# A two-layer graph network: two DRAM tables laid out in four quarters

## The chip, the cores and the metric

The kernel runs on one core of a Trainium2 chip. The metric is the device time of one execution in microseconds. The kernel before takes 4035.39 us, the median of 3 runs (4032.98 to 4035.66).

## The reference

12500 nodes with 256 features, 200000 edges (`src`, `dst`) sorted by `dst`, one weight per edge. Cut to what is computed:

```python
# layer 0: 2 projections, 4 heads of 32, attention-weighted sum over edges, norm per head
feat = relu(einsum('nd,ohdk->ohnk', x, W) + b)
att_s, att_n = leaky(feat[0] . a_self), leaky(feat[1] . a_neigh)
msgs = (att_s[:, row] + att_n[:, col]) * adj_vals * feat[1][:, col, :]
agg = segment_sum(msgs, row)
h0 = concat(norm32([feat[0], agg]) * scale + offset)
x = layernorm(x + h0)
# layer 1: one message per edge, sum over edges, update
messages = relu(concat([x[row], x[col]]) @ W_msg + b_msg)
aggregated = segment_sum(messages, col)
h = relu(concat([x, aggregated]) @ W_upd + b_upd)
x = layernorm(x + layernorm(h) * gamma + beta)
```

In the call `row` is `src` and `col` is `dst` for the first layer's arguments, as `edge_index = stack([src, dst])` is for the second.

## The kernel before

Rows are worked on in 98 tiles of 128 nodes, taken as 49 pairs of 256 rows (`NP` = 49). `x1` below is the x after layer 0. The kernel has three stages; each engine runs its own program, and they meet through semaphores.

The first stage projects the rows and sorts the edges' messages into a DRAM table `d_m`.

The second stage is a loop over `E_END` groups. A group gathers five message rows per partition from `d_m` (L781, by GpSimd's indirect DMA, four buffers `GB`), weighs them (ScalarE L996, VectorE L1753 and L1756) and adds them up by matmul (L1305). Eight groups make a pair. Beside the groups two row pipelines run. `own` makes the first half of the new rows and stores them in `d_xp` (L670). `node`, steps 0 to 21 of a pair after its sums are there, loads them again (step 0, L675, into one of two buffers `X1`; first used at L1849), adds the second half, normalises, and then stores three things. Step 14 (L678) stores the normalised rows plus `bet`, for use as residual, in `d_x1`. Step 15 (L684) stores the transposed rows `XT1` (made at L1042) in `d_y`. Step 17 (L681) stores the product with the first half of `W_msg` in `d_p`. All these DMAs are issued by the SP queue in the order of its program, each after its wait: a late wait holds back all that stand behind it. The step's group is given by the table `AT_B`: one step a group, and for the last pairs two or three steps a group.

At the turn every engine waits in `stored_b` until all stores of `d_xp`, `d_x1`, `d_p` and `d_y` have landed. Only then may the gathers from `d_p` begin.

The third stage is a loop over 403 groups of four gathers (L795, from `d_p`, eight buffers `G1`, so that gathers may run seven groups ahead). VectorE adds the looked-up part of the other end (L1913; the lookup is the matmul L1339), ScalarE applies relu (L1111), the matmul L1327 sums by one-hot, and VectorE adds the sums to `big` (L1903). Beside it runs `node1`, 18 steps for each pair, placed by `AT_F`: step 0 loads the pair's transposed rows (L707, into one of two buffers `XTL`; used by the matmul L1360 in step 2) and, for a pair four ahead, again into `XTQ` (L710, used at L1370 in steps 5 and 6). Step 7 loads the residual rows (L713, buffer `XR`, used by VectorE at L1944 in step 11), and step 17 stores the output (L717). The SP queue also loads the tables of the one-hots, 384 KB every three groups (L698, `spread`).

Both tables are written once and read once or twice. The two shapes on the DRAM side now are

```python
def pair(t, j):
    return t[bass.ds(j * 256, 256), :].rearrange("(b p) c -> p b c", p=128)   # d_x1: 128 x 2 x 1 KB
d_y[p * 128:(p + 1) * 128, :]                                                 # d_y: 128 x 2 KB
```

The SBUF side has 128 partitions in both. If a check of the edges fails, a slow path computes everything in another way; it uses `d_x1` too and does not run here.

Of the kernel before, what the change touches and what calls it, by code (L numbers as in the profile page):

```python
# [15 lines left out]
NP = 49  # L16
# [119 lines left out]
def owned(g):  # L136

    for j in (g // 8 - 1, g // 8):
        if 0 <= j < NP and g - 8 * j < 12:
            yield j, g - 8 * j  # L140
# [24 lines left out]
QL = 4  # L165
# [4 lines left out]
def pq(p, n):  # L170

    return p + min(p, QL) + n
# [7 lines left out]
def dense(g, at):  # L180

    return at.get(g, ())
# [30 lines left out]
def gnn(nc, x, xT, src, dst, ew, srcB, dstB, ewB, dst0, W0, b0, att, scale, offset, Wm, bm, Wu, bu, gam, bet, cst, out):  # L213
    ctx = ExitStack()
    with ctx:
# [5 lines left out]
        def S(name):  # L221
            name = SHARED[name][0] if name in SHARED else name
            if name not in sems:
                sems[name] = ctx.enter_context(nc.semaphore("q_" + name))
            return sems[name]

        def base(name):

            return SHARED[name][1] if name in SHARED else 0

        def waitn(e, name, v):

            if not isinstance(v, int) or v > 0:
                e.wait_ge(S(name), v + base(name))

        def dram(name, shape, dt=f32):
            return nc.dram_tensor(name, shape, dt).ap()
# [12 lines left out]
        d_b = dram("d_b", (3, 768), bf16)  # L250
        d_xp = dram("d_xp", (NROW, 256))
        d_x1 = dram("d_x1", (NROW, 256))
        d_p = dram("d_p", (NROW, 256))
        d_q = dram("d_q", (NROW, 256))
        d_y = dram("d_y", (NP * 128, 512))
        d_loc = dram("d_loc", (NS, 128), bf16)
        srcF, dstF = (t.rearrange("a b -> (a b)").rearrange("(a b c) -> a b c", b=128, c=1) for t in (srcT, dstT))

# [53 lines left out]
        def q4(ap):  # L312
            return ap.rearrange("p (a b) -> p a b", a=4)
# [117 lines left out]
        X1 = [take(2, 256) for _ in range(2)]  # L431
        XN = take(2, 256)
        XT1 = take(4, 128)
# [23 lines left out]
        XTL = [take(4, 128) for _ in range(2)]  # L457
# [5 lines left out]
        XR = scr[:, 4096:4608].rearrange("p (a b) -> p a b", a=2)  # L463
        XTQ = q4(w0[:, :, :].rearrange("p a b -> p (a b)"))
# [25 lines left out]
        def pair(t, j):  # L490

            return t[bass.ds(j * 256, 256), :].rearrange("(b p) c -> p b c", p=128)

        def sm(g, a, n):
            return small[:, g % 4, a:a + n]

# [41 lines left out]
        def stored_b(e):  # L538
            stored_own(e)
            stored_p(e)  # L540
            e.wait_ge(S("b_s1"), 16 * NP)
            e.wait_ge(S("b_s4"), 16 * NP)
# [14 lines left out]
        def _(e):  # L557
# [91 lines left out]
            def columns(j):  # L649

                waitn(e, "d_mm", j - 2)
                n = 256 if j < NP - 1 else 128 + LASTR
                e.dma_start(XT0B[j % 3][:, :, 0:n], xT.rearrange("(k p) n -> p k n", p=128)[:, :, j * 256:j * 256 + n])\
                 .then_inc(S(f"d_xt{j % 3}"), 16)
            columns(0)
            columns(1)
            for g in range(E_END):
                for j, o in owned(g):
                    if o == 0 and j + 2 < NP:
                        columns(j + 2)  # L660
                    if o == 5:
                        waitn(e, f"d_st{j % 2}", 16 * (j // 2))
                        if j < NP - 1:
                            e.dma_start(X0[j % 2], pair(x, j)).then_inc(S(f"d_in{j % 2}"), 16)
                        else:
                            e.dma_start(X0[j % 2][:, 0, :], x[j * 256:j * 256 + 128, :]).then_inc(S(f"d_in{j % 2}"), 16)
                            e.dma_start(X0[j % 2][0:LASTR, 1, :], x[j * 256 + 128:N, :]).then_inc(S(f"d_in{j % 2}"), 16)
                    if o == 11:
                        waitn(e, "d_x", j + 1)
                        e.dma_start(pair(d_xp, j), X0[j % 2]).then_inc(S(f"d_st{j % 2}"), 16)  # L670
                for p, o in dense(g, AT_B):
                    if o == 0:
                        waitn(e, f"d_st{p % 2}", 16 * (p // 2 + 1))
                        waitn(e, "b_s1", 16 * (p - 1))
                        e.dma_start(X1[p % 2], pair(d_xp, p)).then_inc(S(f"b_in{p % 2}"), 16)  # L675
                    if o == 14:
                        waitn(e, "b_xb", p + 1)
                        e.dma_start(pair(d_x1, p), X1[p % 2]).then_inc(S("b_s1"), 16)  # L678
                    if o == 17:
                        waitn(e, "b_pq", pq(p, 0) + 1)  # L680
                        e.dma_start(pair(d_p, p), PB).then_inc(S("b_s3"), 16)  # L681
                    if o == 15:
                        waitn(e, "b_xt", p + 1)
                        e.dma_start(d_y[p * 128:(p + 1) * 128, :], XT1.rearrange("p a b -> p (a b)")).then_inc(S("b_s4"), 16)  # L684
            stored_b(e)
            waitn(e, "b_x", NP)
            waitn(e, "b_mm", pq(NP, 0))
# [7 lines left out]
            def spread(n):  # L695

                waitn(e, "f_ot", BL * (n - 1))
                e.dma_start(LBC[n % 2], d_loc[4 * BL * n:4 * BL * (n + 1), :].rearrange("(o a) b -> o (a b)", o=1).to_broadcast([128, BL * 512]))\  # L698
                 .then_inc(S(f"f_l{n % 2}"), 16)
            spread(0)  # L700
            for g in range(F_END):
                if g % BL == 0 and BL * (g // BL + 1) < NG:
                    spread(g // BL + 1)
                for p, o in dense(g, AT_F):
                    if o == 0:
                        waitn(e, "g_mm", p - 1)
                        e.dma_start(XTL[p % 2].rearrange("p a b -> p (a b)"), d_y[p * 128:(p + 1) * 128, :]).then_inc(S(f"g_in{p % 2}"), 16)  # L707
                        if p + QL < NP:
                            waitn(e, "g_qm", p)
                            e.dma_start(XTQ.rearrange("p a b -> p (a b)"), d_y[(p + QL) * 128:(p + QL + 1) * 128, :]).then_inc(S("g_xq"), 16)  # L710
                    if o == 7:
                        waitn(e, "g_add", p)
                        e.dma_start(XR, pair(d_x1, p)).then_inc(S("g_x"), 16)  # L713
                    if o == 17:
                        waitn(e, "g_n2", 2 * (p + 1))
                        if p < NP - 1:
                            e.dma_start(pair(out, p), UH[p % 3]).then_inc(S(f"g_st{p % 3}"), 16)  # L717
                        else:
                            e.dma_start(out[p * 256:p * 256 + 128, :], UH[p % 3][:, 0, :]).then_inc(S(f"g_st{p % 3}"), 16)
                            e.dma_start(out[p * 256 + 128:N, :], UH[p % 3][0:LASTR, 1, :]).then_inc(S(f"g_st{p % 3}"), 16)  # L720
# [144 lines left out]
        def _(e):  # L865
# [142 lines left out]
            def own(j, o):  # L1008
                if o == 1:
                    waitn(e, "d_mm", j + 1)  # L1010
                    e.activation(FS(j), FS(j), ACT.Relu).then_inc(S("d_re"), 1)
                if o == 5:
                    waitn(e, "d_rv", j)
                    waitn(e, "d_xc", j + 1)
                    e.activation(SQ0, FS(j), ACT.Square).then_inc(S("d_s2"), 1)
                if o == 7:
                    waitn(e, "d_var", j + 1)
                    e.activation(SD(j), sm(j % 2, 56, 8), ACT.Sqrt).then_inc(S("d_sq"), 1)
# [51 lines left out]
            def node1(p, o):  # L1070
# [12 lines left out]
                if o == 7:  # L1083
                    waitn(e, "g_v1", p + 1)
                    e.activation(sm(p, 100, 2), sm(p, 98, 2), ACT.Sqrt).then_inc(S("g_sq"), 1)
                    q = p + QL
                    if q < NP:
                        waitn(e, "g_qm", p + 1)
                        e.activation(big[:, 2 * q + 1:2 * q + 3, :], q2(PG[:, :]), ACT.Copy).then_inc(S("g_qc"), 1)
                if o == 9:  # L1090
                    waitn(e, "g_a1", 2 * (p + 1))
                    waitn(e, "g_rn", p + 1)
                    for b in range(2):
                        e.activation(u[:, b, :], u[:, b, :], ACT.Identity,
                                     bias=sm(p, 104 + b, 1), scale=sm(p, 102 + b, 1)).then_inc(S("g_n1"), 1)
# [1045 lines left out]
```

## Time and profile before

| | us |
|---|---|
| median of 3 timed runs | 4035.39 |
| lowest, highest | 4032.98, 4035.66 |
| span of the profiled execution | 4403.8 |

The profiled execution has no other time than its span, from its first to its last instruction; it is 368.4 us longer than the median of the timed runs. Busy in the span: TensorE 87%, VectorE 77%, ScalarE 63%, GpSimd 56%. A matmul's end is modelled, so TensorE's share is rough. Gathers run on the DMA queue q0 and move 359.18 MB, the SP queue's transfers on q1 and move 343.13 MB. "Share of 16 engines" is the time that the queue's packets took, against 16 DMA engines (here called rings) working all the time; it can pass 100% in a short stretch, since packets overlap. A DMA issue on SP (SPq) is a short instruction; its transfer runs afterwards. Tile names leave out numbers: `d_x` in a row is `d_x1`.

### The profile page before, as it was taken

The page shows a single profiled execution, that of the slowest core. Times are in us where ns is not written, and L with a number is a line of the kernel's source. Part 1 is how long each engine was busy: PE and PEld are TensorE (multiplying, and loading weights), DVE is VectorE, ACT ScalarE, POOL GpSimd, SP SyncE. Part 2 cuts the span into 40 slices and gives each one's busy share as a digit, 9 for nine tenths or more (in the row PEclk, how much of TensorE's full clock was granted, in tenths as well). Part 3 has the DMA queues.
Part 4 walks back from the last instruction along what each step waited for, and adds up shares of the span by engine and source line. Part 5 has one row for each costly group of instructions (what it writes and reads, how often), then busy time and mean ns, then how long its engine had stood idle before and what let it go on. Part 6 is the DMA issues. An engine that isn't in the chain of part 4 may idle for free.

```text
span 4403.8 us, 85804 instructions
## 1 busy us (share of the span) xinstructions
PE 3810.6 (87%) x26341; PEld 3176.6 (72%) x26341; DVE 3380.9 (77%) x7638; ACT 2779.1 (63%) x7247; POOL 2477.9 (56%) x2585
## 2 busy tenths in 40 slices
PE   4999999899999999956888888878888888888886
PEld 4999999788888888845666666666666666666665
DVE  7999999799999999955666666666666666666666
ACT  4888888777777777744555555555555555555554
POOL 2653655344455555536666666666666666666662
PEclk8999999999999999988899999999999989999998
DMA  5776544567777777743444444444444444444442
GB/s 133 243 231 226 190 189 188 197 191 206 209 209 209 209 209 208 206 141 110 127 142 129 136 127 140 132 130 136 131 132 136 135 131 131 128 129 139 131 131 72
DMA packets 344434, 707.82 MB, mean 161 GB/s; under 512 B 58153, under 2 KB 201334, under 8 KB 343954
## 3 DMA queue, kind: packets, MB, share of 16 engines
q0 software_dynamic: 114912, 359.18, 29.2%
q1 hardware_dynamic: 229074, 343.13, 23.1%
q8 instruction: 225, 3.69, 0.4%
q14 instruction: 223, 1.83, 0.1%
HBM read 507.96 MB, written 195.74 MB: 160 GB/s over the span
## 4 chain that ended last, share of the span: by engine, by line
PE 44%; DVE 29%; issue 11%; another core or an unknown queue 9%; ACT 2%; DVEq 2%; DMA 2%; SPq 1%; POOL 0%; ACTq 0%; POOLq 0%
PE ps L1327 11%; PE ps L1339 10%; DVE big L1903 7%; PE ps L1157 6%; DVE scr L1753 4%; PE ps L1305 4%; DVE arena L1913 3%; DVE arena L1756 3%; PE ps L1219 2%; PE ps L1164 2%; PE ps L1230 2%; PE ps L1188 2%; DVE scr L1756 1%; PE ps L1147 1%
## 5 line engine op out<-in xcount | busy, mean ns | idle before, releaser
L795 POOL DMA_INDIRECT arena<-d_p,tabs x1612 | 1543.0, 957 | 890.8 <-issue 457.3
L1913 DVE TENSOR_TENSOR arena<-arena,ps 128x512 f32<-128x512 f32 x806 | 527.0, 683 | 760.9 <-remote 503.8
L1327 PE MATMUL ps<-arena 128*128 128x256 f32 x3224 | 897.3, 419 | 240.1 <-DVE big L1903 174.2
L1111 ACT ACTIVATE arena<-arena 128x1024 f32<-128x1024 f32 x403 | 425.7, 1056 | 1004.8 <-DVE arena L1913 956.3
L1339 PE MATMUL ps<-big,scr 128*128 x3224 | 840.3, 401 | 219.6 <-DVE arena L1913 134.4
L1327 PEld LDWEIGHTS ps<-arena 128*128 128x128 f32 x3224 | 627.7, 205 | 424.2 <-ACT arena L1111 192.3
L1339 PEld LDWEIGHTS ps<-big,scr 128*128 128x128 f32 x3224 | 641.9, 202 | 356.9 <-issue 261.1
L1903 DVE SCALAR_TENSOR_TENSOR big<-big,tabs,ps 128x256 f32 x1612 | 767.8, 476 | 105.7 <-DVE big L1903 47.7
L781 POOL DMA_INDIRECT arena<-d_m,scr x392 | 531.2, 1355 | 564.0 <-DVE arena L1756 220.8
L1305 PE MATMUL ps<-arena,scr 128*128 128x256 f32 x2620 | 614.9, 384 | 10.5 <-DVE arena L1756 10.3
L1305 PEld LDWEIGHTS ps<-arena,scr 128*128 128x128 f32 x2620 | 483.7, 190 | 93.2 <-issue 32.9
L996 ACT ACTIVATE arena<-arena 128x128 f32<-128x128 f32 x1310 | 410.7, 389 | 206.2 <-PE ps L1305 132.7
L1064 ACT ACTIVATE arena<-cstb,tabs 128x128 f32<-128x128 f32 x1612 | 508.8, 386 | 2.3 <-DMA d_p<-arena 2.3
L1157 PE MATMUL ps<-arena,scr 128*128 128x132 bf16 x4860 | 377.0, 221 | 6.5 <-ACT arena L910 4.2
L1753 DVE TENSOR_TENSOR scr<-scr,arena 128x640 f32<-128x640 f32 x392 | 320.7, 818 | 3.2 <-issue 3.1
L1157 PEld LDWEIGHTS ps<-arena,scr 128*128 128x128 bf16 x4860 | 305.1, 97 | 10.5 <-ACT arena L910 6.7
L1305 PE MATMUL ps<-scr 128*128 128x256 f32 x1300 | 307.3, 383 | 3.8 <-DVE scr L1756 3.7
L747 POOL DMA_INDIRECT arena<-d_ts,arena x108 | 135.3, 1253 | 296.0 <-PE ps L1157 274.5
L910 ACT ACTIVATE arena<-ps 128x396 f32<-128x396 f32 x540 | 277.9, 515 | 19.4 <-issue 10.3
L916 ACT ACTIVATE scr<-ps 128x512 bf16<-128x512 f32 (+1 forms) x432 | 251.1, 581 | 52.2 <-PE ps L1164 48.9
L1305 PEld LDWEIGHTS ps<-scr 128*128 128x128 f32 x1300 | 239.6, 190 | 44.3 <-issue 15.2
L1067 ACT ACTIVATE arena<-arena 128x512 f32<-128x512 f32 x403 | 253.8, 630 | 12.7
(285 smaller groups left out, 5753.3 us busy)
## 6 DMA issues: line engine op xcount, KB each, us to landing
d_m<-arena SPq DMA_DIRECT2D x108, 603.0 KB
arena<-d_loc SPq DMA_DIRECT2D x135, 384.0 KB
d_m<-arena SPq DMA_DIRECT2D x108, 402.0 KB
arena<-d_p,tabs POOLq DMA_INDIRECT x1612
arena<-in_xT_dram SPq DMA_DIRECT2D x96, 256.0 KB
d_xp<-arena SPq DMA_DIRECT2D x49, 256.0 KB, 3.3
arena<-d_xp SPq DMA_DIRECT2D x49, 256.0 KB
d_x<-arena SPq DMA_DIRECT2D x49, 256.0 KB
```

The lines of the kernel that those rows point to most:

```text
L781: e.indirect_dma_start(out=GB[g % 4].rearrange("p a b -> p (a b)"), out_offset=None, in_=runs_m, in_offset=bass.IndirectOffsetOnAxis(ap=TI ...
L795: e.indirect_dma_start(out=G1[j % 8][:, k, :], out_offset=None, in_=d_p, in_offset=bass.IndirectOffsetOnAxis(ap=tabS[:, j, k:k + 1], axis= ...
L996: a = e.activation(SW[g % 3][:, s, 0:128], v[:, 0:128], ACT.Copy, scale=v[:, FW + 1:FW + 2])
L1064: s = e.activation(OH1[j % 4][:, k, :], iota, ACT.Square, bias=tabN[:, j, k:k + 1])
L1111: e.activation(G1[g % 8], G1[g % 8], ACT.Relu).then_inc(S("f_re"), 1)
L1157: m = e.matmul(PS[6 + (NE * q + k) % 2][:, (cc - c0) * FW:(cc - c0 + 1) * FW], SELT[q % 2][:, cc, :], FWN[q % 2][:, i * FW:(i + 1) * FW], ...
L1305: m = e.matmul(AC(p)[:, h, :], OHW[g % 3][:, s, :], SW[g % 3][:, s, :], start=first, stop=end)
L1327: m = e.matmul(turn(H, AB)[:, k * 256:k * 256 + 256], OH1[(j - 2) % 4][:, 2 * h + k, :], G1[(j - 2) % 8][:, 2 * h + k, :], start=True, sto ...
L1339: m = e.matmul(turn(H, QB)[:, k * 256:k * 256 + 256], OT1[j % 2][:, 2 * h + k, :], big[:, ts[2 * h + k] + 1, :], start=True, stop=True)
L1753: e.tensor_tensor(OHW[g % 3], IT[t % 3].unsqueeze(1).to_broadcast(b5), v[:, :, FW].unsqueeze(2).to_broadcast(b5), ALU.is_equal).then_inc(S ...
L1903: e.scalar_tensor_tensor(big[:, ts[k], :], big[:, ts[k], :], tabK[:, j - 3, k:k + 1], turn(H, AB)[:, (k % 2) * 256:(k % 2) * 256 + 256], A ...
L1913: e.tensor_tensor(v, v, q2(turn(2 * j + h, QB)[:, :]), ALU.add).then_inc(S("f_m"), 1)
```

## The change

A new DRAM table `d_xr` takes the residual rows in the fast path, `d_x1` stays for the slow path. `d_y` and `d_xr` have the shape [4, 49 * 32, 512]: partitions 0 to 31 of each pair lie in the first quarter, 32 to 63 in the second, and so on. `quarters(t, p)` is the DRAM side of pair p's copy, [4, 32, 512]. The SBUF side is the buffer as [128, 512]; for the residual the two rows of a partition now lie side by side, 2 KB in one piece. The number of stores issued so far is counted in `kept` while the program is written out, and L675 waits for all of them.

```diff
+        d_xr = dram("d_xr", (4, NP * 32, 512))
...
-        d_y = dram("d_y", (NP * 128, 512))
+        d_y = dram("d_y", (4, NP * 32, 512))
...
+        def quarters(t, p):
+
+            return t[:, p * 32:(p + 1) * 32, :]
...
+            kept = 0
...
                     if o == 0:
                         waitn(e, f"d_st{p % 2}", 16 * (p // 2 + 1))
-                        waitn(e, "b_s1", 16 * (p - 1))
+                        waitn(e, "b_s1", 16 * kept)
                         e.dma_start(X1[p % 2], pair(d_xp, p)).then_inc(S(f"b_in{p % 2}"), 16)
                     if o == 14:
                         waitn(e, "b_xb", p + 1)
-                        e.dma_start(pair(d_x1, p), X1[p % 2]).then_inc(S("b_s1"), 16)
+                        kept += 1
+                        e.dma_start(quarters(d_xr, p), X1[p % 2].rearrange("p a b -> p (a b)")).then_inc(S("b_s1"), 16)
...
-                        e.dma_start(d_y[p * 128:(p + 1) * 128, :], XT1.rearrange("p a b -> p (a b)")).then_inc(S("b_s4"), 16)
+                        e.dma_start(quarters(d_y, p), XT1.rearrange("p a b -> p (a b)")).then_inc(S("b_s4"), 16)
...
-                        e.dma_start(XTL[p % 2].rearrange("p a b -> p (a b)"), d_y[p * 128:(p + 1) * 128, :]).then_inc(S(f"g_in{p % 2}"), 16)
+                        e.dma_start(XTL[p % 2].rearrange("p a b -> p (a b)"), quarters(d_y, p)).then_inc(S(f"g_in{p % 2}"), 16)
                         if p + QL < NP:
                             waitn(e, "g_qm", p)
-                            e.dma_start(XTQ.rearrange("p a b -> p (a b)"), d_y[(p + QL) * 128:(p + QL + 1) * 128, :]).then_inc(S("g_xq"), 16)
+                            e.dma_start(XTQ.rearrange("p a b -> p (a b)"), quarters(d_y, p + QL)).then_inc(S("g_xq"), 16)
                     if o == 7:
                         waitn(e, "g_add", p)
-                        e.dma_start(XR, pair(d_x1, p)).then_inc(S("g_x"), 16)
+                        e.dma_start(XR.rearrange("p a b -> p (a b)"), quarters(d_xr, p)).then_inc(S("g_x"), 16)
```

## Rows read from the trace of the kernel before

**Rows 1.** Busy time by stretch: us, then each engine's, clock, DMA share, GB/s.
```profile
821.00:1946.00 1125.00, 1083.98 (x5800) 908.33 (x5800) 1065.71 (x2604) 803.05 (x2566) 531.18 (x393) 0.99 0.69 201
1946.00:4404.00 2458.00, 1975.39 (x7976) 1540.69 (x7976) 1554.18 (x3605) 1336.95 (x2902) 1542.96 (x1612) 0.91 0.43 129
...
1380.00:1822.00 442.00, 436.21 (x2343) 364.76 (x2341) 431.55 (x1063) 324.13 (x1041) 222.96 (x160) 1.00 0.71 209
```

**Rows 2.** Waits: of ScalarE's L996 in 821 to 1946 us, and before L1756.
```profile
ACT arena L996 <- DMA arena<-d_m,scr: 69.1, 60, 8.0
ACT scr L996 <- DMA arena<-d_m,scr: 22.5, 29, 2.2
...
  ACT arena L996: 4.5, 8
  ACT scr L996: 1.5, 4
```

**Rows 3.** SP's DMA issues of one pair: start us, us; then the next pair's first.
```profile
1501.72 0.38 SPq L678 DMA_DIRECT2D d_x<-arena  x1
1503.59 0.38 SPq L670 DMA_DIRECT2D d_xp<-arena  x1
1504.91 0.34 SPq L684 DMA_DIRECT2D d_y<-arena  x1
1506.82 0.38 SPq L675 DMA_DIRECT2D arena<-d_xp  x1
...
1523.80 0.38 SPq L678 DMA_DIRECT2D d_x<-arena  x1
```

**Rows 4.** DMA queue from 32 to 34 us: packets, MB, share of 16 engines.
```profile
q1 hardware_dynamic: 88, 0.04, 7.3%
```

**Rows 5.** The same from 1527 to 1528.5 us.
```profile
q1 hardware_dynamic: 497, 0.58, 107.5%
q0 software_dynamic: 1, 0.00, 0.0%
```

**Rows 6.** Lines L795 and L1913: ns min/median/max, first and last start; L1913's waits.
```profile
L795 POOL DMA_INDIRECT arena<-d_p,tabs x1612: 940/946/1394, 1946.0 to 4339.0; - x180
...
L1913 DVE TENSOR_TENSOR arena<-arena,ps x806: 678/681/690, 1954.6 to 4369.9; 128x512 f32<-128x512 f32 x162
...
  remote: 503.8, 136
  PE ps L1339: 199.1, 106
```

**Rows 7.** Timeline around the last pairs of the second stage; idle time in brackets.
```profile
1923.85 0.40 SPq L678 DMA_DIRECT2D d_x<-arena  x1
1924.62 0.34 SPq L684 DMA_DIRECT2D d_y<-arena  x1
...
1927.79 0.47 SPq L670 DMA_DIRECT2D d_xp<-arena  x1
1930.29 0.38 SPq L675 DMA_DIRECT2D arena<-d_xp  x1
...
1932.95 0.43 DVE L1849 TENSOR_TENSOR arena<-arena 128x256 f32<-128x256 f32 x1 [2.96 <-DMA arena<-d_xp]
...
1937.23 0.37 SPq L678 DMA_DIRECT2D d_x<-arena  x1
1938.46 0.34 SPq L684 DMA_DIRECT2D d_y<-arena  x1
...
1942.98 0.37 SPq L681 DMA_DIRECT2D d_p<-arena  x1
```

**Rows 8.** Timeline of the last two pairs' loads of d_y and their use.
```profile
4358.74 0.47 SPq L707 DMA_DIRECT2D scr<-d_y  x1
...
4361.85 1.13 PE L1360 MATMUL ps<-wut,scr 128*128 128x256 f32 x4 [1.55 <-ACT scr L1076]
...
4383.83 0.47 SPq L707 DMA_DIRECT2D scr<-d_y  x1
...
4386.74 2.05 PE L1360 MATMUL ps<-wut,scr 128*128 128x256 f32 x4 [3.52 <-DMA scr<-d_y]
```

## The prediction

> **What bounds the kernel now.** I read the busy time by stage first [rows 1]. The span has three stages. Sorting lasts to 821 us. The second stage (first layer's edges, and pair by pair the rows of the new x) lasts to 1946 us, and the third (second layer's edges, and pair by pair the output) fills the rest. The change touches only the SP queue's stores in the second stage and its loads in the third. In the steady part of the second stage VectorE works 431.55 of 442 us [rows 1], so it sets the pace. The DMA rings are 71% busy there, the highest of any stage, so this is the place where a slower transfer can hurt. In the third stage the rings are 43% busy and no engine is full; the loop between TensorE, VectorE and ScalarE is the limit.
>
> Then I read who waits for gathers in the second stage. ScalarE's weighing (L996) waits for a landing gather 89 times, 91.6 us in all, and VectorE's product (L1756), which takes ScalarE's result, waits for ScalarE only 12 times, 6.0 us [rows 2]. So lateness of a gather is nearly all absorbed on ScalarE; 6.0 / 91.6 = 6.5% reaches the engine that sets the pace.
>
> Then the SP queue of one pair [rows 3]. The store of the residual rows (L678) is followed 1.87 us later by a store of d_xp (L670), 1.32 us later by the store of transposed rows (L684), and 1.91 us later by a load (L675) that waits for both the d_xp store and the residual stores. A pair takes 1523.80 - 1501.72 = 22.08 us (L678 to L678).
>
> **What the layout does to one transfer.** Both sides of these copies have 128 rows now: 128 partitions and 128 rows of 2 KB in d_y; 128 partitions with two 1 KB pieces each for the residual. Afterwards the DRAM side is [4, 32, 512]. The trace has transfers whose outermost size does not divide into 16: the stores of 101 rows of 512 B in the start-up. In the stretch where one of them runs alone, 0.04 MB move in 2 us at a ring share of 7.3%, about 22 GB/s: one ring of 16 works [rows 4]. Where nothing but transfers of the normal form run, 0.58 MB move in 1.5 us, 387 GB/s on all rings [rows 5]. Nothing shows an outermost size of 4 at this size; the bounds are 16 rings, as now (256 KB / 387 GB/s = 0.68 us), and one ring (256 KB / 22 GB/s = 11.9 us). I take four rings, 88 GB/s: 2.98 us, because the 101-row transfer shows that the shape decides how many rings work. That is 2.3 us longer per transfer, and four rings hold four times the work while twelve hold none.
>
> The Trainium skill (DMA: Bandwidth & Descriptors, section "Why a DMA increments its semaphore by 16 and not by 1") says the same of shapes: the ring count is the largest number up to 16 that divides the slowest dimension of both sides, and on this queue the lowest-numbered rings are used. By that all five changed transfers sit on the same four rings. One ring for 101, a prime, agrees with it; which rings they are no row shows. Its table "Rules for kernel authors" warns against an outermost size below 16, and thus speaks against this change.
>
> The number of transfers is 49 stores of d_xr, 49 stores of d_y, 49 + 45 loads of d_y and 49 loads of d_xr. The residual rows go from 256 pieces of 1 KB to 128 of 2 KB. That saves at best a few tenths of a microsecond of ring time against the 2.3 us added, and I cost it at zero. SP's issue time (0.38 us for L678, 0.34 us for L684 [rows 3]) can move either way by its own size; SP waits for other engines most of the time, so it counts nothing. The new wait of L675 (for all residual stores issued) is the same number as before for all pairs but the last two (after the steps of the last pairs are spread differently, `kept` is p instead of p - 1); queued behind it are the loads of x and x^T and the store of d_p.
>
> **Sum, the ends.** Here a transfer stands on the path.
> - End of the second stage. For the last pair the load L675 (1930.29) follows the d_xp store (1927.79), and VectorE waits 2.96 us for it at 1932.95 [rows 7]. The two long stores before (1923.85 and 1924.62) hold their rings for 2 x 2.98 = 5.96 us after the first begins. The d_xp store comes 3.94 us after the first, so its share on these rings is 2.0 us late. Bounds 0 and 4.6 (both excesses in full). I take 2.0.
> - Turn of the stages. The last two long stores are issued at 1937.23 and 1938.46, and the d_p store for which all gathers wait at 1942.98 [rows 7], 5.75 us after the first: 0.2 us late.
> - End of the kernel. The last load of d_y is issued at 4383.83; TensorE waits 3.52 us and starts at 4386.74 [rows 8], so +2.3. For the pair before, the load is issued at 4358.74 and used at 4361.85, 3.11 us later, after a wait for ScalarE [rows 8]. A load that took 2.91 us takes 5.2: +2.1. Together 4.4, bounds 0 and 4.6.
>
> Ends: 2.0 + 0.2 + 4.4 = 6.6 us.
>
> **Sum, middle of the second stage.** Per pair the SP queue moves seven 256 KB transfers, 7 x 0.68 = 4.8 us of every ring. ScalarE's 91.6 us are 1.87 us per pair, 0.39 us per microsecond of such ring time. The two stores add 4.6 us on four rings, and a gather ends with its slowest ring: 1.8 us more waiting on ScalarE per pair, 88 us over 49 pairs. At today's 6.5% VectorE would feel 6 us. But ScalarE works only 803 of 1125 us [rows 1], its idle time is uneven, and lateness now comes in lumps of 2 to 3 us behind two long stores issued 3.2 us apart. So I take twice that share: 12 us. Bounds: 0 (all hidden) and 225 us (4.6 us x 49, nothing hidden). The load L675 goes out about 2 us later, but its rows are first used at L1849, eight groups of 22.08 / 8 = 2.76 us later, and only the last pair waited [rows 7].
>
> **Sum, middle of the third stage.** The last gather is issued at 4339.0 and the last message made at 4369.9, 30 us later [rows 6]: gathers run some seven groups ahead, so lateness of 2 to 5 us is covered. No VectorE wait for DMA stands among those of L1913. The d_y loads are issued two groups (2 x 2458 / 403 = 12 us) or more ahead of their use, the residual four. I take 0; without the cover it would be up to 3 x 2.3 x 49 = 338 us, which the 30 us of lead excludes for gathers; I leave 20 us of it for the range.
>
> Total +18.6 us, on the profiled span 4403.8 + 18.6 = 4422.4. The profiled execution is 368 us longer than the median of the runs, 4035.39. VectorE's 503.8 us of waits at L1913 that no record explains [rows 6] suggest that recording stretches the third stage; the terms above come from places without such waits, so I carry them over unchanged: 4035.4 + 18.6 = 4054.
>
> **Rivals.**
> - All hidden but the ends: +6.6, 4042. For it: VectorE feels 6.0 us of waits in the whole stage [rows 2]. Against: the two stores fall in the same 3 us of each pair.
> - Gathers starve behind the long stores. Between 1527 and 1528.5 us the SP queue has 107.5% of the rings (modelled) and the gathers' queue 0.0% [rows 5]; if a gather with work waiting gets next to nothing while a store is queued, it is late by the whole of the excess. From the point where lateness passes what ScalarE has in hand, VectorE stalls each pair. A third of the 4.6 us getting through is 75 us, 4117 with the ends. The Trainium skill (DMA: Bandwidth & Descriptors, "Queues, rings and completion order") has rings served in turn by packets of some 9 to 17 descriptors; by that a gather gives way to large pieces of a store at each of its own packets, which is this rival. Whether a gather was waiting in the stretch these rows don't show.
> - Faster: what delays a gather today is not its ring but the memory or the ports behind all rings, and a store at 88 instead of 387 GB/s disturbs less. Two of seven transfers are changed, 2/7 of 91.6 us = 26 us, 4009 at full effect. It decides if gathers beside the long stores wait less than they do now. Against: a gather needs all its rings.
> - The split is not made on the outermost size: times as before, 4035. Against: rows 4.
>
> **How the numbers follow.** Chances: forecast 0.46 (own range 4043 to 4085), all hidden but the ends 0.20, starving 0.13, faster 0.14, no split 0.07. A measurement tells about 0.2%, 8 us, from no change. The second and last case fall within that; of the forecast nearly all is above. Slower 0.60, same 0.26, faster 0.14. The range 4025 to 4120 leaves out most of the faster case and the tail of the starving one.
>
> **What would show it.** The ring share of a stretch around L684 falls to about a quarter while the store runs. L675 is issued 1 to 3 us later after L670 than now. ScalarE's waits for gathers at L996 rise from 91.6 to about 180 us, VectorE's at L1756 from 6 to about 20. The wait of L1360 for the last d_y load grows from 3.52 to about 5.8 us. The third stage's groups keep their pace. I am wrong if the store's bandwidth stays near 387 GB/s, if VectorE's busy share in the second stage falls by more than 5 points, or if the third stage moves by over 1%.

## The result and the profile after

The changed kernel takes 4079.15 us (median of 4 runs, 4074.53 to 4084.18), the kernel before 4034.18 us (4030.78 to 4035.66) on the same chip: ratio 1.0109, interval 1.0097 to 1.0121, or 45 us more. The forecast was 4054, 18.6 us more.

The profile that the prediction was made from has a span of 4403.8 us. On one chip of the experiments every kernel that ran there takes some 350 us longer, nearly all of it in the third stage (below), and a profile of the kernel before taken there (span 4393.0) looks like that one; so I take the first profile to come from such a chip; which chip it was is not on record. For the third stage I therefore compare with a second profile of the kernel before, taken on a chip of the normal speed (span 4032.5). In the second stage the two profiles of before agree to 2 us.

Busy time by stretch of this second profile of before: second stage from the sixth to the 44th pair (start of L1867), its end up to the first gather of the third stage, the third stage's middle up to the last message, and the rest. Columns as in [rows 1].
```profile
1015.70:1854.50 838.80, 828.13 (x4450) 693.51 (x4449) 818.96 (x2016) 616.16 (x1978) 423.22 (x305) 1.00 0.71 209
1854.50:1948.00 93.50, 71.10 (x330) 57.83 (x328) 70.53 (x180) 48.65 (x149) 21.16 (x18) 0.89 0.50 151
1948.00:3998.60 2050.60, 1851.23 (x7940) 1453.51 (x7941) 1532.88 (x3563) 1328.46 (x2887) 1553.24 (x1612) 0.98 0.51 154
3998.60:4032.50 33.90, 11.09 (x38) 7.34 (x36) 13.96 (x43) 7.60 (x16) 0.00 (x0) 0.70 0.10 31
```
The same four stretches of the changed kernel, in a profile taken on the same chip as that one (span 4075.2):
```profile
1015.50:1877.10 861.60, 831.76 (x4449) 696.14 (x4448) 823.25 (x2016) 612.96 (x1978) 413.40 (x305) 1.00 0.68 203
1877.10:1979.60 102.50, 70.69 (x330) 57.82 (x328) 70.69 (x180) 49.11 (x152) 21.15 (x18) 0.89 0.46 138
1979.60:4037.90 2058.30, 1858.19 (x7939) 1471.34 (x7940) 1527.89 (x3562) 1326.28 (x2887) 1555.65 (x1612) 0.96 0.54 154
4037.90:4075.20 37.30, 12.11 (x39) 8.05 (x37) 14.00 (x43) 7.61 (x16) 0.00 (x0) 0.65 0.08 28
```
The differences are +22.8, +9.0, +7.7 and +3.4 us, 42.9 in all (the start adds -0.2). The first profile of the changed kernel (span 4077.3) gives 26.2, 7.1, 7.0 and 3.8 for the same four. So three quarters of the loss lie in the second stage. GpSimd and ScalarE are not busier there; VectorE is short of work: it idles 38.4 us of 861.6, before 19.8 of 838.8.

What VectorE waits for in the second stage's middle is in the groups of its three products. Before (second profile): operation, shapes, count | busy us, mean ns | idle before it.
```profile
L1753 DVE TENSOR_TENSOR scr<-scr,arena 128x640 f32<-128x640 f32 x304 | 248.1, 816 | 0.1
L1756 DVE TENSOR_TENSOR arena<-arena 128x640 f32<-128x640 f32 x203 | 165.7, 816 | 0.0
L1756 DVE TENSOR_TENSOR scr<-scr,arena 128x640 f32<-128x640 f32 x101 | 82.4, 816 | 0.0
```
After (the lines are 7 further down; same profile as the stretches above):
```profile
L1760 DVE TENSOR_TENSOR scr<-scr,arena 128x640 f32<-128x640 f32 x304 | 248.2, 816 | 3.3 <-DMA arena<-d_m,scr 3.0
L1763 DVE TENSOR_TENSOR arena<-arena 128x640 f32<-128x640 f32 x203 | 165.9, 817 | 7.1 <-ACT arena L1003 6.7
L1763 DVE TENSOR_TENSOR scr<-scr,arena 128x640 f32<-128x640 f32 x101 | 82.6, 818 | 8.2 <-ACT scr L1003 8.0
```
Idle time goes from 0.1 to 18.6 us (21.1 in the first profile), of the 22.8 that this stretch grew. The other 4.3 are VectorE's busy time in the stretch (818.96 to 823.25 us), while none of its groups is longer by more than 0.2; perhaps instructions that follow each other overlap a little in the records and after a wait don't. That is argued and not shown.

ScalarE's weighing waits 208.7 us for gathers in the second stage, before 91.6 [rows 2]. (First profile, waits from 821 to 1982 us: total, times, longest.)
```profile
ACT arena L1003 <- DMA arena<-d_m,scr: 137.6, 71, 8.0
...
ACT scr L1003 <- DMA arena<-d_m,scr: 71.1, 39, 4.6
```

The timeline at the end of the second stage, in the first profile as are the next rows, answers to [rows 7].
```profile
1953.89 0.52 SPq L685 DMA_DIRECT2D d_xr<-arena  x1
...
1954.65 0.52 SPq L691 DMA_DIRECT2D d_y<-arena  x1
...
1957.39 0.40 SPq L688 DMA_DIRECT2D d_p<-arena  x1
...
1957.84 0.49 SPq L676 DMA_DIRECT2D d_xp<-arena  x1
...
1964.76 0.38 SPq L681 DMA_DIRECT2D arena<-d_xp  x1
1967.55 0.43 DVE L1856 TENSOR_TENSOR arena<-arena 128x256 f32<-128x256 f32 x1 [7.54 <-DMA arena<-d_xp]
...
1971.84 0.52 SPq L685 DMA_DIRECT2D d_xr<-arena  x1
...
1973.06 0.52 SPq L691 DMA_DIRECT2D d_y<-arena  x1
...
1977.36 0.38 SPq L688 DMA_DIRECT2D d_p<-arena  x1
```
From the d_xp store to the load that reads it back are 6.92 us (before 2.50), and VectorE waits 7.54 us for that load (before 2.96). And the last load of d_y, which answers to [rows 8]:
```profile
4053.52 0.52 SPq L714 DMA_DIRECT2D scr<-d_y  x1
...
4059.17 2.04 PE L1367 MATMUL ps<-wut,scr 128*128 128x256 f32 x4 [6.28 <-DMA scr<-d_y]
```

The transfer's rate is as forecast. From 1975 to 1977 us only the last pair's two long stores are on the queue; the DMA view of this stretch says (packets, MB, share of 16 engines):
```profile
q1 hardware_dynamic: 91, 0.18, 25.7%
```
The view gives 92 GB/s for it, on a quarter of the rings; the forecast took 88. The two stores together last longer than 2 x 2.98 us, though: the first of their 256 packets of 2 KB starts at 1972.99 and the last ends at 1980.11, 7.1 us, because the first 2 us of it move only some 30 packets.

### The profile page after: what moved, and what is told of

Read it like the earlier page. It is cut to its first block, busy times and chain, and to the rows that moved or that the text cites. A ratio compares the mean times of both kernels' runs of the same rounds, so it can differ in the third digit from the quotient of the medians.

```text
span 4077.3 us, 85804 instructions
## 1 busy us (share of the span) xinstructions
PE 3701.8 (91%) x26341; PEld 3104.5 (76%) x26341; DVE 3374.8 (83%) x7638; ACT 2771.2 (68%) x7247; POOL 2478.6 (61%) x2585
## 4 chain that ended last, share of the span: by engine, by line
PE 33%; POOL 26%; DVE 12%; issue 12%; DMA 12%; ACT 4%; SPq 1%; DVEq 0%; ACTq 0%; POOLq 0%
POOL arena L802 26%; PE ps L1164 7%; PE ps L1312 6%; DMA arena<-d_m,scr 5%; DMA arena<-d_p,tabs 5%; PE ps L1334 4%; PE ps L1346 3%; DVE scr L1760 2%; PE ps L1226 2%; DVE arena L1763 2%; PE ps L1171 2%; PE ps L1195 2%; PE ps L1237 2%; ACT arena L1003 2%; PE ps L1154 2%
## 5 line engine op out<-in xcount | busy, mean ns | idle before, releaser
L1346 PE MATMUL ps<-big,scr 128*128 x3224 | 801.8, 388 | 155.4 <-DVE arena L1920 143.2
L788 POOL DMA_INDIRECT arena<-d_m,scr x392 | 521.8, 1331 | 603.0 <-DVE arena L1763 252.7
L1334 PE MATMUL ps<-arena 128*128 128x256 f32 x3224 | 835.0, 395 | 53.6 <-DVE big L1910 49.5
L1346 PEld LDWEIGHTS ps<-big,scr 128*128 128x128 f32 x3224 | 612.7, 193 | 274.3 <-issue 191.4
L1334 PEld LDWEIGHTS ps<-arena 128*128 128x128 f32 x3224 | 587.9, 192 | 223.5 <-DVE big L1910 92.8
L1003 ACT ACTIVATE scr<-arena 128x128 f32<-128x128 f32 x650 | 203.6, 388 | 105.1 <-DMA arena<-d_m,scr 71.1
```

Of the source, the lines that this page charges most:

```text
L788: e.indirect_dma_start(out=GB[g % 4].rearrange("p a b -> p (a b)"), out_offset=None, in_=runs_m, in_offset=bass.IndirectOffsetOnAxis(ap=TI ...
L1003: a = e.activation(SW[g % 3][:, s, 0:128], v[:, 0:128], ACT.Copy, scale=v[:, FW + 1:FW + 2])
L1334: m = e.matmul(turn(H, AB)[:, k * 256:k * 256 + 256], OH1[(j - 2) % 4][:, 2 * h + k, :], G1[(j - 2) % 8][:, 2 * h + k, :], start=True, sto ...
L1346: m = e.matmul(turn(H, QB)[:, k * 256:k * 256 + 256], OT1[j % 2][:, 2 * h + k, :], big[:, ts[2 * h + k] + 1, :], start=True, stop=True)
```

## Experiments

Theory after the result: the long stores delay the gathers beside them beyond what these have in hand, and that alone is the second stage's loss; the long loads cost the rest. Rivals: the layout in DRAM or the longer pieces are the cause; the load of d_xp waits on SP for the residual store; a fixed share of every delay gets through.

The first four kernels ran on the chip where the kernel before takes 4385.59 us (25 runs), the rest on chips where it takes 4033.21 (20 runs) and 4034.23 (10 runs). Each ratio is to the kernel before on the same chip.

**The kernel before, unchanged.** (No edit.)

> The kernel before, unchanged, for a second profile. If the 327 us by which the third stage of the first profile is longer than that of the changed kernel came from the profiling of that one execution, the third stage (first L795 gather to the end) here takes about 2087 us (4033 - 1946) instead of 2458, and L1913's waits have a releaser. If that stage is really so long, the span is 4400 again. Time: 4035, ratio 1.000 within 0.1%.

Measured: 4382.4, ratio 0.9996 [0.9982, 1.0010]. The time of 4035 that I expected is missed by the chip and not by the kernel; the third stage really is that long here, in the timed runs as in the profile (span 4393.0).

**Sixteen parts.** Both tables [16, 49 * 8, 512].
```diff
-        d_xr = dram("d_xr", (4, NP * 32, 512))
+        d_xr = dram("d_xr", (16, NP * 8, 512))
-        d_y = dram("d_y", (4, NP * 32, 512))
+        d_y = dram("d_y", (16, NP * 8, 512))
-            return t[:, p * 32:(p + 1) * 32, :]
+            return t[:, p * 8:(p + 1) * 8, :]
```

> The changed kernel with both tables in sixteen parts, [16, 49 * 8, 512], instead of four: the copies stay scattered in DRAM and the residual stays in 2 KB pieces, but the outermost size is 16. Theory of rings (an outermost size of four leaves a transfer on four rings, and gathers behind it are late): all of the loss goes, 4033 +- 6, first gather of the third stage at about 1946 us. Theory of layout (scattered parts, 2 KB pieces or the table's place in memory cost the time): the loss stays, 4075 to 4080.

Measured: 4390.39, ratio 1.0008 [0.9999, 1.0018]. Here the rows are strewn over more parts, and the residual pieces are 2 KB as in the changed kernel. Neither costs or brings anything that can be measured (the second stage's middle takes 839.5 us, before 839.3); what is left is the outermost size. The changed kernel itself did not run on this chip; that the loss is there too is seen from the next run.

**Only d_y in quarters** (the residual as before):
```diff
-                        e.dma_start(quarters(d_xr, p), X1[p % 2].rearrange("p a b -> p (a b)")).then_inc(S("b_s1"), 16)
+                        e.dma_start(pair(d_x1, p), X1[p % 2]).then_inc(S("b_s1"), 16)
-                        e.dma_start(XR.rearrange("p a b -> p (a b)"), quarters(d_xr, p)).then_inc(S("g_x"), 16)
+                        e.dma_start(XR, pair(d_x1, p)).then_inc(S("g_x"), 16)
```

> Only the table of transposed rows in quarters; the residual rows as before. Rings: a pair has one long store in the second stage instead of two. Half of the loss if it adds up, 4057; less if lateness is absorbed up to a point, about 4045. Theory that the wait of the load L675 for the residual stores is what costs: those stores are as short as before here, so 4037 or less.

Measured: 4414.65, ratio 1.0056 [1.0036, 1.0076]. That is about half of the changed kernel's 1.0109 to 1.0120.

**Only the residual in quarters** (d_y as before):
```diff
-        d_y = dram("d_y", (4, NP * 32, 512))
+        d_y = dram("d_y", (NP * 128, 512))
```
with its store and loads on `d_y[p * 128:(p + 1) * 128, :]`.

> Only the table of residual rows in quarters; transposed rows as before. Rings: one long store a pair again, 4045 to 4057. Theory of the wait at L675: nearly the whole loss stays, 4070 to 4080. With the run that has only the transposed rows in quarters it tells whether the two losses add (sum 45) or only the pair of stores close together costs (sum well under 45).

Measured: 4386.96, ratio 0.9999 [0.9985, 1.0014]: none of the 10 to 22 us that I expected. Yet SP stands as long for the residual store in front of the load of d_xp as in the changed kernel: 158.0 us in 45 waits, there 159.6 in 47, before 60.3 in 39. That wait is real and costs nothing; the rival that made it the cause falls. The costs of the two tables don't add up either: in the middle of the second stage the profiles show +14.8 us with d_y alone, +1.8 with the residual alone (both against the unchanged kernel on the same chip), +26.2 or +22.8 with both.

**The changed kernel again**, as control for the next three.

> The changed kernel again, as the control for the three beside it. If the ratio is the same on a chip whose third stage takes 2450 us as on one with 2090, it is 1.011 (4434 against 4386 there, 4079 against 4034 here). If the third stage with its slower pace covers its loads, only the 36 us of the second stage are left: 1.008 there.

Measured: 4079.07, ratio 1.0120 [1.0102, 1.0138].

**The store of d_y six steps later**, some 13 us away from the residual's:
```diff
-                    if o == 15:
+                    if o == (21 if p < NP - 5 else 15):
+                        if o == 21:
+                            waitn(e, "e_d", 8 * p + 32)
```

> The changed kernel, but the store of the transposed rows is issued in the quiet part of a pair: after the load of x^T, and once TensorE has done the pair's 32nd group (8 groups a pair), not right behind the store of d_xp. Only pairs below 44. The store is as long as before, on the same rings. Rings, with lateness that counts only from a point on: the gathers issued beside it have over 4 us in hand, the middle of the second stage loses 2 us or less instead of 26, the first gather of the third stage comes at about 1958 us instead of 1982: 24 us less than the changed kernel. Theory that the amount of ring time alone costs: no change against the changed kernel.

Measured: 4045.93, ratio 1.0035 [1.0021, 1.0049]: 33 of the 46 us are gone, with the same four-ring stores. VectorE's products in this kernel (its lines stand 2 further down; 1014.2 to 1853.4 us):
```profile
L1762 DVE TENSOR_TENSOR scr<-scr,arena 128x640 f32<-128x640 f32 x304 | 248.2, 816 | 0.1
L1765 DVE TENSOR_TENSOR arena<-arena 128x640 f32<-128x640 f32 x203 | 165.7, 816 | 0.0
L1765 DVE TENSOR_TENSOR scr<-scr,arena 128x640 f32<-128x640 f32 x101 | 82.5, 816 | 0.3 <-ACT scr L1005 0.3
```
And its ScalarE in the same stretch:
```profile
ACT arena L1005 <- DMA arena<-d_m,scr: 109.9, 88, 3.6
ACT scr L1005 <- DMA arena<-d_m,scr: 45.8, 36, 2.6
```
The same rows of the changed kernel (second profile, 1015.5 to 1877.1 us):
```profile
ACT arena L1003 <- DMA arena<-d_m,scr: 101.9, 64, 4.4
ACT scr L1003 <- DMA arena<-d_m,scr: 64.7, 34, 4.6
```
This is the reading that matters most here. ScalarE waits 155.7 us for gathers in one kernel and 166.6 in the other, nearly the same; VectorE feels 0.4 us of the first and 18.6 of the second. With d_y alone in quarters ScalarE waits 157.4 us, and VectorE feels 12.4. So the sum of ScalarE's waits does not tell what reaches VectorE. What differs is where the lateness falls. The gather queue's data packets, cut in order into 64 for each gather, give the time from a gather's issue to its last packet. The mean in us over gathers 49 to 352, by place in the pair (a column's number is the gather's issue, in us after that of the residual's store; it is the same in all rows to within 0.4 us; the two rows with one table alone in quarters come from the slower chip, where the kernel before gives 4.5, 5.8, 5.2, 4.0, 3.6 and 4.5):

| kernel | 2.3 | 5.8 | 8.3 | 11.8 | 14.0 | 16.7 | VectorE idle before its products, us |
|---|---|---|---|---|---|---|---|
| before (second profile) | 4.5 | 5.7 | 5.3 | 4.0 | 3.6 | 4.5 | 0.1 |
| residual alone in quarters | 6.3 | 5.6 | 5.6 | 4.3 | 3.7 | 4.4 | 1.5 |
| eight parts (next) | 6.7 | 6.2 | 5.6 | 4.1 | 3.6 | 4.4 | 1.9 |
| changed, d_y late | 5.6 | 5.5 | 5.5 | 4.2 | 3.6 | 5.6 | 0.4 |
| d_y alone in quarters | 7.2 | 6.4 | 5.8 | 4.4 | 3.5 | 4.5 | 12.4 |
| changed (second profile) | 6.8 | 7.1 | 6.6 | 5.1 | 4.3 | 4.3 | 18.6 |
| two parts (below) | 7.1 | 5.6 | 5.8 | 5.5 | 5.7 | 5.3 | 33.1 |

In the changed kernel four gathers in a row are late, by 2.3, 1.3, 1.2 and 1.0 us (from the unrounded means), and of VectorE's 18.5 us of idle time before the products of groups 49 to 352 (gaps over 0.1 us) 11.7 stand at the second of them and 2.4 at the first. With d_y late the lateness falls on two places far apart, 1.1 us each (and 0.7 at the gather behind the second), and only 0.4 us reaches VectorE. A single gather late by 1.8 or 2.2 us (residual alone, eight parts) costs next to nothing either; one late by 2.7 (d_y alone) does, and most of the idle time stands at it (10.4 us). So there is a reserve of a little over 2 us, and gathers that are late one behind the other use it up together. That the reserve is ScalarE's idle time between groups fits this, and is argued.

**Eight parts.** (The edit of sixteen, with 8 and 16 rows.)

> Tables in eight parts, [8, 49 * 16, 512]. Rings: a transfer works on eight rings for 1.4 us instead of four for 3.0 us; an excess of 0.7 us is within what is in hand, so the middle of the second stage loses 0 to 4 us, first gather of the third stage at 1948 to 1955 us, ratio 1.001 to 1.003. If cost goes with the excess (2.3 -> 0.7 us), a third of the loss, 1.0035.

Measured: 4039.7, ratio 1.0019 [1.0009, 1.0029]. From 1943.5 to 1944.5 us:
```profile
q1 hardware_dynamic: 79, 0.16, 45.2%
```

**The kernel before, once more**, on the chip of these runs.

> The kernel before again, for its profile on this chip. On a chip where it takes 4034 us, the third stage takes 2087 us and gathers are issued 5.0 us a group with VectorE waiting for their landing, as in the changed kernel's profile; the changed kernel's 2095 us then mean that its third stage loses about 8 us. On a chip where it takes 4385 us nothing new.

Measured: 4033.28, ratio 1.0001 [0.9991, 1.0010]. It gave the second profile of before.

**Short loads, long stores.** Each load of the third stage in four transfers of 32 rows:
```diff
-                        e.dma_start(XTL[p % 2].rearrange("p a b -> p (a b)"), quarters(d_y, p)).then_inc(S(f"g_in{p % 2}"), 16)
+                        for q in range(4):
+                            e.dma_start(XTL[p % 2][q * 32:(q + 1) * 32, :, :].rearrange("p a b -> p (a b)"), d_y[q, (p) * 32:(p) * 32 + 32, :]).then_inc(S(f"g_in{p % 2}"), 16)
...
-                    waitn(e, f"g_in{p % 2}", 16 * (p // 2 + 1))
+                    waitn(e, f"g_in{p % 2}", 64 * (p // 2 + 1))
```
and the same for XTQ and XR, with their waits.

> The stores of both tables keep the changed form (outermost size 4); each load of the third stage is issued as four transfers of 32 rows of one quarter, so that none has an outermost size of four (and SP issues 4 x 143 of them instead of 143). Theory: the profiles put 32 to 34 of the change's 45 us into the second stage and about 11 into the third, and the 11 come from the long loads (3.5 us at the end of the kernel, 5 to 8 us in the third stage's middle). Then this kernel takes before + 34, about 4067 (ratio 1.0085), its third stage lasts 2084 to 2087 us from the first gather to the end as in the kernel before (2084.5), and TensorE's wait for the last rows of d_y at L1367 is back at 5 us. Rival: the third stage's 11 us are not the loads (the scatter of one profiled execution, or the later start); then the time stays at before + 45, 4079 (1.011). If the extra 429 issues on SP cost something, it is slower than either.

Measured: 4070.01, ratio 1.0096 [1.0079, 1.0113], before + 35.8. The third stage takes 2087.7 us from the first gather to the end (before 2084.5, changed 2095.6). TensorE's waits for d_y are not quite back at 5 us, but at 7.6 in all (before 5.2, changed 10.5). They are two waits, for the last two pairs' loads. The first of them in the second profile of before, and in that of the changed kernel:
```profile
3990.56 1.10 PE L1360 MATMUL ps<-wut,scr 128*128 128x256 f32 x4 [1.70 <-DMA scr<-d_y]
```
```profile
4027.88 2.04 PE L1367 MATMUL ps<-wut,scr 128*128 128x256 f32 x4 [4.51 <-DMA scr<-d_y]
```
In the first profile of the changed kernel it is 6.26 us, with short loads 3.40.

**Short stores, long loads.** The mirror image, with the waits for `b_s1` and `b_s4` at four times their counts:
```diff
-                        e.dma_start(quarters(d_y, p), XT1.rearrange("p a b -> p (a b)")).then_inc(S("b_s4"), 16)
+                        for q in range(4):
+                            e.dma_start(d_y[q, p * 32:(p + 1) * 32, :], XT1[q * 32:(q + 1) * 32, :, :].rearrange("p a b -> p (a b)")).then_inc(S("b_s4"), 16)
```

> The mirror image: loads as in the changed kernel (outermost size 4), each of the two stores of a pair issued as four transfers of 32 rows of one quarter. Theory: the second stage's loss comes from the long stores alone, so the first gather of the third stage is back at about 1948 us (changed kernel 1980 to 1982), VectorE's waits at L1763 for ScalarE are below 6 us, and what is left is the loads' part: before + 9 to 11, 4043 (ratio 1.0025). SP issues six more transfers a pair, 6 x 0.35 = 2.1 us of 22; if that delays the loads of x and d_xp, up to 10 us more. Rival, the number of rings is not what delays the gathers, but the layout (where the quarters lie in DRAM) or the residual landing later for SP: then the time stays at before + 34 or more, 4067 to 4079.

Measured: 4044.85, ratio 1.0027 [1.0015, 1.0039], before + 10.6. The first gather of the third stage is at 1946.3 us (before 1948.0), and the middle of the second stage is that of the kernel before to the tenth:
```profile
1013.60:1852.40 838.80, 828.10 (x4450) 693.54 (x4449) 818.95 (x2015) 615.24 (x1978) 423.26 (x305) 1.00 0.71 209
```
The tables lie in quarters here as in the changed kernel, and SP issues six transfers more a pair. So neither the layout nor SP's issue time costs anything in this stretch; the few rings of the stores do. And the two halves add up: 35.8 + 10.6 = 46.4, measured together 45.9.

**Two parts.** (The edit of sixteen, with 2 and 64 rows.)

> Both tables in two halves ([2, 49 * 64, 512]) instead of four quarters: with one ring for each part a transfer would take 2 x 2.98 = 5.96 us, 5.3 us longer than on 16 rings (four parts: 2.3 us longer). Threshold theory (lateness costs nothing up to what a gather has in hand, and all of it beyond): the two stores of a pair exceed by 10.6 us instead of 4.6, and what was 0.68 us a pair becomes up to 0.68 + 6.0 = 6.7, so the second stage grows by 38 x 6.7 = 250 us in its middle (bounds 150 to 330), 4033 + 250 + 30 = about 4310. Proportional rival (a fixed share of the excess gets through): 0.68 x 10.6 / 4.6 = 1.6 us a pair, 60 us in the middle, with twice the ends and the third stage's part about 4033 + 60 + 2.3 x 19 = 4137. If four parts did not take four rings but something else, the time does not follow the number of parts.

Measured: 4104.7, ratio 1.0173 [1.0156, 1.0190], before + 70.5, less than either theory gave. The transfer runs as slowly as assumed; from 1996 to 1997.5 us:
```profile
q1 hardware_dynamic: 34, 0.07, 12.7%
```
VectorE's products, 1016.7 to 1894.1 us:
```profile
L1760 DVE TENSOR_TENSOR scr<-scr,arena 128x640 f32<-128x640 f32 x304 | 248.3, 817 | 8.1 <-DMA arena<-d_m,scr 7.7
L1763 DVE TENSOR_TENSOR arena<-arena 128x640 f32<-128x640 f32 x203 | 165.9, 817 | 15.8 <-ACT arena L1003 15.7
L1763 DVE TENSOR_TENSOR scr<-scr,arena 128x640 f32<-128x640 f32 x101 | 82.5, 817 | 9.2 <-ACT scr L1003 9.2
```

| tables | share of 16 rings, alone | VectorE's idle time before its products, us | second stage's middle | time against before |
|---|---|---|---|---|
| as before | 102.3% | 0.1 | 0 | 0 |
| 8 parts | 45.2% | 1.9 | +2.4 | +6.5 |
| 4 parts, d_y late | | 0.4 | +0.4 | +12.7 |
| 4 parts | 25.7% | 18.6 to 21.1 | +22.8 to 26.2 | +45.9 |
| 2 parts | 12.7% | 33.1 | +38.6 | +70.5 |

From eight parts to four the middle's loss grows tenfold, from four to two by a half to two thirds. My threshold theory had its lower half right and its upper half wrong: above the threshold the stall does not grow by the full excess. By the packets of the gather queue (table above), the gather beside the stores lands after 7.1 us, only 0.3 us later than with four parts (6.8), although each store takes twice as long. The longer stores reach further gathers instead: those issued 11.8, 14.0 and 16.7 us after the residual's store are late by 1.5, 2.1 and 0.9 us, and of VectorE's idle time, 31.0 us counted as above, 25.8 stand at the one of 11.8.

By the Trainium skill (DMA: Bandwidth & Descriptors, "Queues, rings and completion order") a ring takes its queues in turn, a packet of descriptors at a time. By that a gather would be held up once for each packet of its own on a busy ring, however long the store is; that the gather beside the stores loses 2.3 us with four parts and 2.6 with two agrees with this. The turns themselves are in no row here, so the explanation stays argued.

## Why the prediction was wrong

The direction, the place and the first link (few rings, so late gathers) were right. How much of the lateness reaches VectorE was not, and with it the size: +18.6 forecast, +45 measured. By its own terms:

- **Transfer time: right in the rate.** 88 GB/s taken, 92 measured, on a quarter of the rings; but a pair's two stores, taken as 5.96 us, lasted 7.1. By the rule of the Trainium skill (DMA: Bandwidth & Descriptors, "Why a DMA increments its semaphore by 16 and not by 1") the outermost size 8, 4 and 2 should engage as many rings; 45.2, 25.7 and 12.7% of 16 agree, the first a little under a half.
- **Middle of the second stage: mis-sized, 12 us taken, 23 to 26 measured.** This is the larger part of the error. The step that failed is "so lateness of a gather is nearly all absorbed on ScalarE; 6.0 / 91.6 = 6.5% reaches the engine that sets the pace". These 6.0 us of VectorE's waits [rows 2] all lie before 1015 us, in the stage's start; in its middle VectorE waited 0.0 us (the rows of before above). A share taken from a start-up says nothing of the steady part. There ScalarE's waits for gathers grew from 74.2 to 166.6 us and VectorE's idle time from 0.1 to 18.6, a fifth of it; and no share would hold: the y-late kernel shows 155.7 us on ScalarE for 0.4 on VectorE. What the runs show in its place is the reserve of some 2 us that several late gathers in a row use up. The sign that I named for it, ScalarE from 91.6 to about 180 and VectorE from 6 to about 20, was nearly met (208.7, and 14.5 + 8.8 = 23.3), but even by it the term should have been 14 and not 12, and the direct waits for gathers at L1753 (from 0.1 to 3.3 and 4.6 us) were left out.
- **End of the second stage and turn: 2.2 us taken, 7.1 to 9.0 measured.** For the last pair the load of d_xp came 6.92 - 2.50 = 4.42 us later against its store, and VectorE waited 7.54 - 2.96 = 4.58 us more. That is as much as the upper bound of 4.6; in the two second profiles it was 7.4 - 3.3 = 4.1. I had let the d_xp store begin 3.94 us after the first long one and counted only what of that was left. The packets show what was wrong: the two long stores lasted from 1955.04 to 1963.03 us, 8.0 and not 5.96, with the pieces of a d_p store that I had left out and of the d_xp store between theirs, and the last of these pieces ended at 1964.40, 1.4 us behind them and 0.4 before L681 (before: L675) was issued. The turn's 0.2 was 1.3 to 1.8 (from the last L1867 to the first gather: 9.07 and 9.46 us before, 10.80 and 10.85 after): the d_p store, for which all gathers wait, stands behind both long stores in the same way. The rest of the 7.1 to 9.0 us I can't put down to a wait.
- **Middle of the third stage: 0 taken, 7 to 8 measured.** I left 20 us of room for it, but the reason for the zero was false. "Gathers run some seven groups ahead" holds on the chip of that profile only, and so does what I said of the profiler: "recording stretches the third stage" is wrong, since an execution of the same program on another chip, recorded as well, shows no such waits, and on the slow chip the timed runs are as long as the recorded one (last section). At normal speed the last gather is issued at 3991.2 us and the last message made at 3998.6, 7.4 us later and not 30, and the gathers are what the third stage waits for. Of the 7 to 8 us, 2.8 to 4.6 stand in one place: TensorE's wait for the last pair but one's load of d_y, which falls in this stretch and was 1.70 us before, 4.51 and 6.26 after. The rest, 2 to 5 us, stays open. The profiles don't order it by the length of the loads (the middle takes 2.3 us more than before with short loads, 4.8 with long loads and short stores, 7.0 with eight parts and 9.7 with two), VectorE's waits for gathers do not rise (343.1 us before, 333.6 after), and TensorE's granted clock in this stretch, 0.98 before, is 0.96 to 0.98 in the four profiles with four-part loads at this speed and 0.98 with two parts.
- **End of the kernel: place right, size a little small.** 4.4 us taken for two loads. TensorE's wait for the last one grew by 6.28 - 3.52 = 2.76 us, forecast 2.3 (this stretch grew by 3.4 and 3.8 in all); that for the one before grew by 2.8 and 4.6, forecast 2.1, and stands in the stretch above. Together the two waits grew by 5.3 and 7.3 us (5.2 before, 10.5 and 12.5 after), over the bound of 4.6.
- **The new wait of L675 at nothing, the pieces of 2 KB at nothing: right**, by the residual-only and the sixteen-part kernels.

The sum of the two profiles is 42.9 and 44.1 us, of 45 timed. Of the rivals, "gathers starve" had the second link right (past what ScalarE has in hand, VectorE stalls each pair) and the first too strong: the gather beside the stores is late by 2.3 us and not by the whole excess of 4.6, and by 2.6 when the stores take twice as long. Its price took a third of every excess; 0.6 us a pair got through (22.8 / 38), an eighth. "Faster" and "no split" are out by the 45 us and by the 25.7%.

No kernel here beats the kernel before. Sixteen parts and the residual alone in quarters equal it within the measurement.

## What to carry to other kernels

Before you price a delay by the share of past delays that reached the pacing engine, ask the trace where in the stage these waits lie, and read the time in hand of each transfer that will be late, one behind the other: the reserve is a step and not a slope, so the same store moved to a quiet place cost nothing in the middle. Here one long store a pair was free for the residual and cost half of the loss for d_y, and both close together cost more than the sum; in eight parts the loss was a seventh. And where the profiled execution is much longer than the timed runs, don't build a cover on the stretch that is longer: in the second profile, as long as the timed runs, it was not there.

## What the runs showed that I had not expected

One program took 4033 us on one chip and 4386 on another, with both values repeatable (lowest to highest 4028 to 4039 and 4371 to 4404). The stretch that differs is the third stage. The third stage of the kernel before on the slow chip, and then on the normal one (columns as in [rows 1]):
```profile
1948.80:4393.00 2444.20, 1978.04 (x7976) 1541.08 (x7976) 1554.94 (x3605) 1340.14 (x2902) 1546.82 (x1612) 0.91 0.44 130
```
```profile
1948.00:4032.50 2084.50, 1862.32 (x7976) 1460.85 (x7976) 1546.84 (x3605) 1336.07 (x2903) 1553.24 (x1612) 0.97 0.51 152
```
All engines do the same work; TensorE is granted 0.91 instead of 0.97 and is busy 116 us longer, a third of the 359.7. What L1913 waits for is another thing, too. On the slow chip:
```profile
  remote: 430.7, 145
  PE ps L1339: 252.6, 103
```
On the normal one:
```profile
  DMA arena<-d_p,tabs: 343.1, 188
  PE ps L1339: 54.5, 36
```
There the gathers are far ahead and groups stall for something the records don't name; on the normal one the gathers set the pace. What that something is stays open.
